# Thirteen single rows per group on SyncE's queue and nine ungathered tiles in a graph-attention kernel

## The chip, the cores and the metric

The kernel runs on one core of one Trainium2 chip. The metric is the device time of one launch in microseconds (us). Before the change the median of three runs is 999.71 us (999.69 to 1000.49).

## What is computed

One layer of graph attention over 6250 nodes and 100000 edges, sorted by destination node, with a residual and a layer norm. Cut to what matters:

```python
Q_h, K_h, V_h = x @ Wq + bq, x @ Wk + bk, x @ Wv + bv      # 6250 nodes, 8 heads of 12
E = edge_attr @ We + be                                     # 100000 edges
score = K_h[src] * Q_h[dst] / sqrt(12) * E
score = exp(clip(score.sum(-1), -5, 5))
wV = segment_sum(V_h[src] * score, dst)                     # edges are sorted by dst
Z = segment_sum(score, dst)
out = layernorm(x + wV / (Z + 1e-6))
```

## The kernel before

The edges are cut into tiles of 128 and the tiles into 99 groups, numbered 0 to 98: 97 groups of eight tiles, then one of four and one of two. Each engine runs the whole series of groups in its own program, unrolled, and semaphores hold the engines together. First a short stage computes K and V for every node and stores them as rows of 768 bytes in a table in DRAM (`kv_table`); Q goes to a second table through the SBUF tensor `q_full`, which nobody uses once the query table is written.

What each engine does per group g:

- **GpSimd (POOL)** gathers K and V of the source nodes: one indirect DMA of 128 rows per tile (line 419), into `kv`, a ring of eight groups. Groups 0 to 3 take another route. Before group g it waits until VectorE has ended group g-8, and from group 16 on also for `q_done` to reach g-1, which is TensorE's end of the query product of group g-2.
- **TensorE (PE)** turns the edge product of group g+1 (line 522), computes the edge projection (line 501) and the query product (line 511) of group g+2, and then sums group g (line 571). The turn of group g+1 needs VectorE's `qe` of g+1.
- **VectorE (DVE)** begins group g with the product of keys and queries (line 944), which needs `kv` of g. Right behind it in its order stands `qe` of group g+1 (line 861), then the reduction, the clip, the messages, and small steps of the layer norm.
- **ScalarE (ACT)** takes the exponential of group g and copies the edge projection of g+2.
- **SyncE (SP)** issues the plain loads. Its turn for group g begins when the query product of g is done (`q_done`, line 355). It then issues two query windows for g+4 (line 244), the edge features of g+4 (line 233) and a row of relations for g+8 (line 228). In every fourth turn, at multiples of four, it first reads eight window bases into registers (line 238), and also issues the load of the residual rows (line 319); in the turn after that it issues the store of an output block (line 330).

Five tiles are not gathered: the last tile of groups 24, 40, 56, 72 and 88 (`BY_ROW`). Their 128 rows are loaded one by one by SP, eight rows at the end of each of 16 successive turns, in turns 7 to 86 (`load_single_rows`, called on line 375): one register load of the eight source nodes (line 341), then eight DMAs of one row each (line 345), into a buffer `kv_rows`. In ACT's program, at the end of group g-1, stands a wait for all 128 rows of group g and a copy of the tile to its place in `kv` (line 696); DVE waits for that copy ahead of line 944 of group g.

Of the kernel before, what the change touches and what calls it, by code (L numbers as in the profile page):

```python
# [4 lines left out]
P = 128  # L5
N = 6250
E = 100000
D = 96
# [12 lines left out]
EPS_LN = 1e-5  # L21
U = 8
CLOSE = 2 * U
BY_ROW = (24, 40, 56, 72, 88)
ROWS = 8
XG = 4
TURNS = NB // U
KV_CHUNKS = (4, 6, 10, 10, 8, 6, 4, 2)
# [33 lines left out]
def gnn_program(nc, xT, xrows, src, src_row, dst_group, dst_tile, eaT, w_node, w_edge, out):  # L62
    f32, bf16, i32 = mybir.dt.float32, mybir.dt.bfloat16, mybir.dt.int32
    ALU, ACT, AX = mybir.AluOpType, mybir.ActivationFunctionType, mybir.AxisListType

    kv_table = nc.dram_tensor("kv_table", (NR, 2 * D), f32, kind="Internal").ap()
# [6 lines left out]
    with ctx:  # L73
        def sb(name, shape, dt):
            return ctx.enter_context(nc.sbuf_tensor(name, shape, dt))
# [23 lines left out]
        q_full = sb("q_full", [P, NR // P, D], f32)  # L99
# [27 lines left out]
        idx = sb("idx", [P, NG * T], i32)  # L127
        ea = sb("ea", [DA, EAR, GE], f32)
        row_id = sb("row_id", [1, len(BY_ROW) * P], i32)
        kv_rows = sb("kv_rows", [P, len(BY_ROW), 2 * D], f32)  # L130
        qwin = sb("qwin", [P, QRING, 2, D], bf16)
        place = sb("place", [P, 2, T, PW], f32)
        qke = sb("qke", [P, T, D], f32)
# [30 lines left out]
        kv_mm, kv_up, kv_out = sem("kv_mm"), sem("kv_up"), sem("kv_out")  # L164
# [8 lines left out]
        row_id_in, rows_up = sem("row_id_in"), sem("rows_up")  # L173
# [30 lines left out]
        def alone(at, t):  # L204

            return at in BY_ROW and t == T - 1

        def engine_turns(eng, body, unrolled):

# [14 lines left out]
        def edge_pass(first):  # L224
# [23 lines left out]
            with nc.Block() as block:  # L248

                @block.sync  # L250
                def _(sp):
# [80 lines left out]

                    ahead = []

                    def load_single_rows(turn):

                        i, j = turn // (P // ROWS), turn % (P // ROWS)
                        if turn == 0:
                            sp.wait_ge(row_id_in, 16)
                            sp.wait_ge(kv_out, 16 * len(KV_CHUNKS))  # L340
                        nodes = nc.values_load_multi_w_load_instructions(
                            row_id[0:1, i * P + j * ROWS:i * P + (j + 1) * ROWS], engines=[sp.engine], min_val=0,
                            max_val=N - 1, skip_runtime_bounds_check_because="source nodes of edges are nodes")[1]
                        for p in range(ROWS):
                            sp.dma_start(kv_rows[j * ROWS + p:j * ROWS + p + 1, i], kv_table[bass.ds(nodes[p], 1), :]
                                         ).then_inc(rows_in[i], 16)

                    def loads(r, k, at):


                        if at >= NG:
                            return
                        g, j, q, half = U * r + k, at % BG, U // BG * r + k // BG, k // BG % 2
                        sp.wait_ge(q_done, g + 1)
                        sp.sem_inc(loads_begun, 1)
                        if j == 0 and at + QRING < NG:
                            ahead[:] = window_rows(sp, g + QRING, min(BG, NG - at - QRING))
                        if at + QRING < NG:
                            load_windows(sp, k % QRING, ahead[2 * j:2 * j + 2])
                        if at + EAR < NG:  # L360
                            load_ea(sp, g + EAR, k % EAR)
                        if at + RELR < NG:
                            load_rel(sp, g + RELR, k % RELR)
                        if not first:
                            return
                        if j == 0 and at < NB:
                            if at >= 2 * BG:
                                sp.wait_ge(block_steps, BLOCK_STEPS * q - 2 * BLOCK_STEPS + 4)
                                sp.sem_inc(stores_begun, 1)
                            load_rows(q, half)  # L370
                        if j == 1 and at >= 2 * BG:
                            store_rows(q - 2, half, at)
                        turn = at - (BY_ROW[0] - P // ROWS - 1)
                        if 0 <= turn < len(BY_ROW) * P // ROWS:
                            load_single_rows(turn)

                    engine_turns(sp, loads, first)
                    if first:
# [334 lines left out]
                def _(dve):  # L713
# [202 lines left out]
                    def arithmetic(r, k, at):  # L916

                        if at == NG:
                            return
                        g = U * r + k  # L920
                        s = k % 2
                        nt = tiles(at)

                        def between(place):


                            step = BLOCK_PLACES.get((at % BG, place))
                            if not first or at < BG or step is None:
                                return
                            if step == BLOCK_STEPS and at >= 3 * BG:  # L930
                                dve.wait_ge(ob_out, 16 * (U // BG) * r + 16 * (k // BG) - 32)
                            block_step(step, U // BG * r + k // BG - 1, 1 - k // BG, BC, xb_in[1 - k // BG], r + k // BG)

                        dve.wait_ge(t_done, g + 1)
                        if first and at < XG:
                            dve.wait_ge(conv_up, T // 2 * (k + 1))
                        else:
                            fills = r if first and k < XG else r + 1
                            singles = sum(1 for x in BY_ROW if first and x <= at and x % U == k)
                            dve.wait_ge(kv_in[k], 16 * (T * fills - (T - nt) - singles))  # L940
                            if first and at in BY_ROW:
                                dve.wait_ge(rows_up, BY_ROW.index(at) + 1)
                        by_bank = dict(b=2, t=nt // 2)
                        nc.vector.tensor_tensor(  # L944
                            qke[:, 0:nt].rearrange("p (t b) d -> p b t d", **by_bank),
                            psT[:, :, 0:nt // 2 * D].rearrange("p b (t d) -> p b t d", d=D),
                            kv[:, k, 0:nt, 0:D].rearrange("p (t b) d -> p b t d", **by_bank),
                            ALU.mult).then_inc(qke_done, 1)
                        if 0 < at < NG - 1:
                            make_qe(r, k + 1, at + 1)  # L950
                        between(0)
                        dve.wait_ge(qke_done, g + 1)
                        nc.vector.tensor_reduce(logit[:, 0:nt * H],  # L953
                                                qke[:, 0:nt].rearrange("p t (h d) -> p (t h) d", h=H), AX.X, ALU.add).then_inc(logit_done, 1)
                        between(1)
                        if at >= 2:
                            dve.wait_ge(wt_done, g - 1)
                        dve.wait_ge(logit_done, g + 1)
                        nc.vector.tensor_scalar(clipped[:, s, 0:nt * H], logit[:, 0:nt * H], -5.0, 5.0, ALU.max,  # L959
                                                ALU.min).then_inc(clip_done, 1)  # L960
                        between(2)
                        if at + 1 < NG and at != NG - 2:
                            make_place(r, k + 1, at + 1)
                        between(3)
                        if at >= 2:
                            dve.wait_ge(sum_done, g - 1)
                        dve.wait_ge(wt_done, g + 1)
                        nc.vector.tensor_copy(weight[:, 0:nt * H].rearrange("p (t h) -> p t h", t=nt),  # L968
                                              msg[:, s, 0:nt, D:ML]).then_inc(weight_held, 1)
                        dve.wait_ge(weight_held, g + 1)  # L970
                        nc.vector.tensor_tensor(  # L971
                            msg[:, s, 0:nt, 0:D].rearrange("p t (h d) -> p t h d", h=H),
                            kv[:, k, 0:nt, D:2 * D].rearrange("p t (h d) -> p t h d", h=H),
                            weight[:, 0:nt * H].rearrange("p (t h) -> p t h", t=nt).unsqueeze(3)
                            .broadcast_to([P, nt, H, HD]), ALU.mult).then_inc(msg_done, 1)
                        if at == NG - 2:
                            make_place(r, k + 1, at + 1)
                        between(4)
                        if at == 0:
                            make_qe(r, k + 1, at + 1)  # L980
                        if at + 3 < NG:
                            make_pick(r, k + 3, at + 3)
                        between(5)
# [122 lines left out]
```

## Time and profile before

| | |
|---|---|
| median of three runs | 999.71 us |
| the profiled execution's own time | 999.58 us |
| its span in the profile | 997.9 us |
| POOL busy | 741.4 us, 74% |
| DVE busy | 651.9 us, 65% |
| PE busy | 646.7 us, 65% |
| ACT busy | 186.5 us, 19% |
| DMA engines, mean busy share | about 0.6 from 150 us on |

The profiled execution is 0.13 us below the median; its span is 1.68 us shorter than its own time. Busy shares count an engine's own work alone. SP has no busy share, since issuing DMAs and loading registers isn't counted; its work is seen in the timeline of its queue. In the timeline, times are microseconds from the start of the span, and a line's second number is how long the merged instructions took.

### The profile page before, as it was taken

What the parts mean: (1) busy time and instruction counts of PE and PEld (TensorE: products, weight loads), DVE (VectorE), ACT (ScalarE), POOL (GpSimd) and SP (SyncE); (2) the same over time, 40 slices, a digit from 0 to 9 for tenths busy, and PEclk for the clock granted to TensorE, in tenths of its full rate; (3) what the DMA queues carried; (4) which work ended last, traced back from release to release, by engine and by line L of the source; (5) the groups of instructions that cost most, each with busy time, mean ns of one, the idle gap of its engine ahead of it and who ended that gap; (6) DMA issues with size and microseconds to landing.
All of it is one profiled execution on the core that took longest, in us unless ns stands there. A gap on an engine that the chain in (4) does not pass through costs nothing. (4 is left out here: it accounts for less than half of the span.)

```text
span 997.9 us, 13968 instructions
## 1 busy us (share of the span) xinstructions
PE 646.7 (65%) x3276; PEld 418.5 (42%) x3276; DVE 651.9 (65%) x1307; ACT 186.5 (19%) x373; POOL 741.4 (74%) x783
## 2 busy tenths in 40 slices
PE   5688778656655665748566666567657664757663
PEld 5564555433433443435333343344434443434443
DVE  6637999666756665766565766566756666657665
ACT  4742222111111111111111111111111111111111
POOL 7777777777777777777777777777777777777772
PEclk9888999888877887886878787877887788887885
DMA  6899776665656556555656556565565565665531
GB/s 196 286 293 244 197 203 176 177 184 156 176 143 170 155 146 177 156 153 159 168 145 167 148 147 171 152 162 156 157 176 142 145 174 149 162 160 140 143 86 42
DMA packets 102425, 165.62 MB, mean 166 GB/s; under 512 B 45725, under 2 KB 65006, under 8 KB 102335
## 3 DMA queue, kind: packets, MB, share of 16 engines
q1 hardware_dynamic: 64399, 84.88, 30.8%
q0 software_dynamic: 36784, 74.86, 28.6%
q10 hardware_dynamic: 1152, 4.92, 1.4%
q8 instruction: 28, 0.46, 0.2%
q14 instruction: 62, 0.51, 0.2%
HBM read 152.18 MB, written 12.39 MB: 165 GB/s over the span
## 5 line engine op out<-in xcount | busy, mean ns | idle before, releaser
L419 POOL DMA_INDIRECT kv<-kv_table,idx x745 | 709.8, 953 | 227.1 <-issue 225.9
L522 PE MATMUL psT<-identity,qe 96*128 96x96 f32 x782 | 111.8, 301 | 292.0 <-DVE qe L861 291.9
L944 DVE TENSOR_TENSOR qke<-psT,kv 128x768 f32<-128x768 f32 (+1 forms) x99 | 93.6, 945 | 288.6 <-DMA kv<-kv_table,idx 287.1
L501 PE MATMUL psE<-ea,we 97*96 97x512 f32 x392 | 268.8, 825 | 0.8 <-ACT kv L641 0.8
L522 PEld LDWEIGHTS psT<-identity,qe 96*128 96x128 f32 x782 | 89.2, 172 | 308.6 <-DVE qe L861 308.4
L571 PEld LDWEIGHTS psA<-place,msg 128*104 128x104 f32 x1536 | 159.9, 179 | 36.0 <-DVE msg L971 26.0
L571 PE MATMUL psA<-place,msg 128*104 128x104 f32 x1536 | 167.0, 264 | 9.9 <-DVE msg L971 9.5
L671 ACT ACTIVATE qe<-psE 96x1024 f32<-96x1024 f32 (+1 forms) x99 | 99.8, 1009 | 231.2 <-PE psE L501 231.2
L685 ACT ACTIVATE msg<-clipped 128x64 f32<-128x64 f32 (+1 forms) x99 | 25.3, 255 | 513.4 <-DVE clipped L959 503.4
L861 DVE TENSOR_TENSOR qe<-psQ,qe 96x1024 f32<-96x1024 f32 (+1 forms) x99 | 118.5, 1197 | 3.7 <-ACT qe L671 3.6
L501 PEld LDWEIGHTS psE<-ea,we 97*96 97x96 f32 x392 | 77.8, 224 | 82.8 <-issue 82.8
L849 DVE TENSOR_TENSOR place<-psI,rel_tile 128x832 f32<-128x832 f32 (+1 forms) x99 | 98.1, 991 | 0.0
L971 DVE TENSOR_TENSOR msg<-kv,psI 128x768 f32<-128x768 f32 (+1 forms) x99 | 93.4, 943 | 3.4
L953 DVE TENSOR_REDUCE logit<-qke 128x64 f32<-128x768 f32 (+1 forms) x99 | 91.4, 924 | 0.0
L511 PE MATMUL psQ<-q_parts,qwin 126*96 126x512 bf16 x196 | 71.3, 450 | 1.2 <-DMA qwin<-q_table 1.2
L511 PEld LDWEIGHTS psQ<-q_parts,qwin 126*96 126x96 bf16 x196 | 30.7, 157 | 87.4 <-issue 85.2
L840 DVE TENSOR_SCALAR q_parts<-q_parts,query_id 126x1024 bf16<-126x1024 bf16 x99 | 50.3, 508 | 15.3 <-DMA q_parts<-rel_table 15.3
L417 POOL DMA_INDIRECT xg<-xrows,idx x32 | 31.0, 969 | 11.1 <-issue 9.4
L959 DVE TENSOR_SCALAR clipped<-logit 128x64 f32<-128x64 f32 (+1 forms) x99 | 21.2, 215 | 4.7
L532 PE MATMUL psA<-identity,accT 104*128 104x104 f32 x73 | 14.8, 312 | 14.4 <-ACT accT L679 13.9
L913 DVE TENSOR_SCALAR ob<-psI,stat,spread 128x96 f32<-128x96 f32 x73 | 23.0, 369 | 0.0
L968 DVE COPY psI<-msg 128x64 f32<-128x64 f32 (+1 forms) x99 | 21.4, 216 | 2.0 <-ACT msg L685 1.9
(105 smaller groups left out, 324.9 us busy)
## 6 DMA issues: line engine op xcount, KB each, us to landing
ea<-eaT SPq DMA_DIRECT2D x99, 384.0 KB, 4.1
q_parts<-rel_table SPq DMA_DIRECT2D x99, 252.0 KB
kv<-kv_table,idx POOLq DMA_INDIRECT x745
kv_rows<-kv_table SPq DMA_DIRECT2D x640, 0.8 KB
qwin<-q_table SPq DMA_DIRECT2D x198, 23.6 KB
xb<-xrows SPq DMA_DIRECT2D x24, 144.0 KB
out<-ob SPq DMA_DIRECT2D x24, 144.0 KB
kv_table<-kv ACTq DMA_DIRECT2D x2, 960.0 KB, 8.3
```

Source lines behind the costliest of these rows:

```text
L419: pool.indirect_dma_start(kv[:, k, t], None, kv_table, sources).then_inc(kv_in[k], 16)
L501: last = nc.tensor.matmul(psE[0:D, h, 0:size], we[:], ea[:, k % EAR, edge:edge + size], start=True, stop=True)
L511: last = nc.tensor.matmul(psQ[0:D, h, 0:size], qwin[0:QR, k % QRING, h], pick[0:QR, k % 2, h * GE // 2:h * GE // 2 + size], start=True, st ...
L522: last = nc.tensor.transpose(psT[:, t % 2, t // 2 * D:(t // 2 + 1) * D], qe[0:D, k % 2, t * P:(t + 1) * P], identity[0:D, 0:D])
L571: last = nc.tensor.matmul(sums[0:ML, off:off + PW], msg[:, s, t], place[:, s, t], start=opens, stop=closes)
L671: nc.scalar.activation(qe[0:D, k % 2, 0:edges], psE[0:D].rearrange("d b e -> d (b e)")[:, 0:edges], ACT.Copy).then_inc(e_up, 1)
L840: nc.vector.tensor_scalar(pick[0:QR, k % 2], rel[0:QR, k % RELR], query_id[0:QR], None, ALU.is_equal).then_inc(pick_done, 1)
L849: nc.vector.tensor_tensor(place[:, k % 2, 0:nt], ps_ids.unsqueeze(1).broadcast_to([P, nt, PW]), rel_tile[:, bass.ds(g * T, nt)].unsqueeze( ...
L861: nc.vector.tensor_tensor(qe[0:D, k % 2, 0:edges], psQ[0:D].rearrange("d b e -> d (b e)")[:, 0:edges], qe[0:D, k % 2, 0:edges], ALU.mult). ...
L944: nc.vector.tensor_tensor(qke[:, 0:nt].rearrange("p (t b) d -> p b t d", **by_bank), psT[:, :, 0:nt // 2 * D].rearrange("p b (t d) -> p b ...
L953: nc.vector.tensor_reduce(logit[:, 0:nt * H], qke[:, 0:nt].rearrange("p t (h d) -> p (t h) d", h=H), AX.X, ALU.add).then_inc(logit_done, 1)
L971: nc.vector.tensor_tensor(msg[:, s, 0:nt, 0:D].rearrange("p t (h d) -> p t h d", h=H), kv[:, k, 0:nt, D:2 * D].rearrange("p t (h d) -> p t ...
```

## The change

- `BY_ROW` is now the last tile of groups 15, 25, 35, ..., 95: nine tiles and not five.
- SP's turns load 13 rows and not 8 (the tenth turn of a tile loads the 11 that are left), so that a tile takes ten turns. They run in turns 4 to 93: turns 4 to 13 load the tile of group 15, turns 14 to 23 that of group 25, and so on. The wait for the table, which stands ahead of the first of them, moves with it from turn 7 to turn 4.
- `kv_rows` lies in `q_full`'s memory.
- POOL's gathers of line 419 go from 745 to 741.
- DVE's wait count for the copy is written as a sum; it means the same.

```diff
-BY_ROW = (24, 40, 56, 72, 88)
-ROWS = 8
+SP_ROWS = 13
+SP_TURNS = -(-P // SP_ROWS)
+FROM = 4
+SP_TILES = tuple(15 + SP_TURNS * i for i in range(9))
+BY_ROW = SP_TILES
...
-        kv_rows = sb("kv_rows", [P, len(BY_ROW), 2 * D], f32)
+        kv_rows = q_full[:].rearrange("p t d -> p (t d)").rearrange("p (i f) -> p i f", f=2 * D)[:, 0:len(BY_ROW)]
...
+        def load_single_rows(eng, i, j, rows):
+
+            count = min(rows, P - j * rows)
+            edge = i * P + j * rows
+            nodes = nc.values_load_multi_w_load_instructions(
+                row_id[0:1, edge:edge + count], engines=[eng.engine], min_val=0, max_val=N - 1,
+                skip_runtime_bounds_check_because="source nodes of edges are nodes")[1]
+            for p in range(count):
+                eng.dma_start(kv_rows[j * rows + p:j * rows + p + 1, i], kv_table[bass.ds(nodes[p], 1), :]
+                              ).then_inc(rows_in[i], 16)
...
-                        turn = at - (BY_ROW[0] - P // ROWS - 1)
-                        if 0 <= turn < len(BY_ROW) * P // ROWS:
-                            load_single_rows(turn)
+                        turn = at - FROM
+                        if turn == 0:
+                            sp.wait_ge(row_id_in, 16)
+                            sp.wait_ge(kv_out, 16 * len(KV_CHUNKS))
+                        if 0 <= turn < len(SP_TILES) * SP_TURNS:
+                            load_single_rows(sp, turn // SP_TURNS, turn % SP_TURNS, SP_ROWS)
...
-                                dve.wait_ge(rows_up, BY_ROW.index(at) + 1)
+                                dve.wait_ge(rows_up, sum(1 for x in BY_ROW if x <= at))
```

## Rows read from the trace of the kernel before

**Rows 1.** Page, costliest groups: out<-in xcount | busy, mean ns | idle before, releaser.
```profile
L419 POOL DMA_INDIRECT kv<-kv_table,idx x745 | 709.8, 953 | 227.1 <-issue 225.9
L944 DVE TENSOR_TENSOR qke<-psT,kv 128x768 f32<-128x768 f32 (+1 forms) x99 | 93.6, 945 | 288.6 <-DMA kv<-kv_table,idx 287.1
```
**Rows 2.** Timeline of POOL: gathers 97, 121, 200, 732; first of groups 16, 19, 29, 96.
```profile
166.57 0.95 POOL L419 DMA_INDIRECT kv<-kv_table,idx  x1 [0.30 <-issue]
...
196.56 0.94 POOL L419 DMA_INDIRECT kv<-kv_table,idx  x1 [0.30 <-issue]
...
295.89 0.95 POOL L419 DMA_INDIRECT kv<-kv_table,idx  x1 [0.30 <-issue]
...
963.03 0.95 POOL L419 DMA_INDIRECT kv<-kv_table,idx  x1 [0.30 <-issue]
```
**Rows 3.** SP's instructions by line: duration ns min/median/max, first and last start.
```profile
L345 SPq DMA_DIRECT2D kv_rows<-kv_table x640: 224/228/288, 116.1 to 871.1; - x160
L341 SPq TENSOR_LOAD <-row_id x80: 526/631/838, 114.8 to 866.8; - x80
L318 SPq TENSOR_LOAD <-block_int x24: 446/462/619, 76.3 to 927.6; - x24
L696 ACT ACTIVATE kv<-kv_rows x5: 350/351/352, 254.6 to 891.3; 128x192 f32<-128x192 f32 x5
```
**Rows 4.** Timeline of SP's queue: turns 4 to 8, turns 13 and 14, and the last of turn 23.
```profile
97.33 0.89 SPq L244 DMA_DIRECT2D qwin<-q_table  x2
98.27 1.79 SPq L233 DMA_DIRECT2D ea<-eaT  x1
100.10 0.41 SPq L228 DMA_DIRECT2D q_parts<-rel_table  x1
101.53 0.37 SPq L319 DMA_DIRECT2D xb<-xrows  x1
102.16 0.87 SPq L244 DMA_DIRECT2D qwin<-q_table  x2
...
103.50 0.40 SPq L228 DMA_DIRECT2D q_parts<-rel_table  x1
106.09 0.84 SPq L244 DMA_DIRECT2D qwin<-q_table  x2
...
112.99 0.85 SPq L244 DMA_DIRECT2D qwin<-q_table  x2
...
114.30 0.41 SPq L228 DMA_DIRECT2D q_parts<-rel_table  x1
116.05 3.15 SPq L345 DMA_DIRECT2D kv_rows<-kv_table  x8
122.26 0.87 SPq L244 DMA_DIRECT2D qwin<-q_table  x2
...
160.45 0.85 SPq L244 DMA_DIRECT2D qwin<-q_table  x2
...
164.66 3.17 SPq L345 DMA_DIRECT2D kv_rows<-kv_table  x8
168.08 0.83 SPq L244 DMA_DIRECT2D qwin<-q_table  x2
...
237.73 3.17 SPq L345 DMA_DIRECT2D kv_rows<-kv_table  x8
```
**Rows 5.** The same view: window loads of turns 12, 16 and 20.
```profile
153.19 0.86 SPq L244 DMA_DIRECT2D qwin<-q_table  x2
...
183.15 0.89 SPq L244 DMA_DIRECT2D qwin<-q_table  x2
...
213.67 0.86 SPq L244 DMA_DIRECT2D qwin<-q_table  x2
```
**Rows 6.** Waits of SP's queue: us in total, times, longest.
```profile
SPq L355 <- PE psQ L511: 253.8, 57, 12.0
```
**Rows 7.** Timeline: DVE's line 944 of groups 4, 15, 16; PE's line 511 of 17.
```profile
100.41 0.95 DVE L944 TENSOR_TENSOR qke<-psT,kv 128x768 f32<-128x768 f32 x1
...
170.85 0.95 DVE L944 TENSOR_TENSOR qke<-psT,kv 128x768 f32<-128x768 f32 x1
...
175.42 0.60 PE L511 MATMUL psQ<-q_parts,qwin 126*96 126x512 bf16 x2
...
179.88 0.96 DVE L944 TENSOR_TENSOR qke<-psT,kv 128x768 f32<-128x768 f32 x1 [3.34 <-DMA kv<-kv_table,idx]
```
**Rows 8.** The same: line 944 of group 22, line 511 of group 24.
```profile
240.15 0.96 DVE L944 TENSOR_TENSOR qke<-psT,kv 128x768 f32<-128x768 f32 x1 [5.90 <-DMA kv<-kv_table,idx]
...
247.03 0.64 PE L511 MATMUL psQ<-q_parts,qwin 126*96 126x512 bf16 x2
```
**Rows 9.** The same: line 944 of groups 95 to 98.
```profile
964.55 0.96 DVE L944 TENSOR_TENSOR qke<-psT,kv 128x768 f32<-128x768 f32 x1 [3.31 <-DMA kv<-kv_table,idx]
974.48 0.96 DVE L944 TENSOR_TENSOR qke<-psT,kv 128x768 f32<-128x768 f32 x1 [4.00 <-DMA kv<-kv_table,idx]
980.25 0.54 DVE L944 TENSOR_TENSOR qke<-psT,kv 128x384 f32<-128x384 f32 x1
983.42 0.35 DVE L944 TENSOR_TENSOR qke<-psT,kv 128x192 f32<-128x192 f32 x1
```
**Rows 10.** Page, DMA issues: KB each, median us to landing.
```profile
ea<-eaT SPq DMA_DIRECT2D x99, 384.0 KB, 4.1
xlast<-xrows SPq DMA_DIRECT2D x1, 48.0 KB, 2.0
```

More of the change, by code:

```diff
@@ L333, in _ @@
                     ahead = []
[L335 to L346, printed above, removed]
                     def loads(r, k, at):
```

## The prediction

> **What bounds the kernel now.** I read the costliest groups first. POOL's gathers are busy for 709.8 us, and every gap before one is "issue": POOL waits for nobody. Line 944 is DVE's only large wait, 287.1 us, and what ends it is the landing of a gather [rows 1]. So the pace is POOL's. The timeline of POOL says how fast that is: from the first gather of group 19 to the first of group 96 there are 611 gathers in 963.03 - 196.56 = 766.47 us, which is 1.254 us each [rows 2]. A gather less is 1.25 us less, as long as nothing makes POOL wait.
>
> This pace doesn't hold from the start. DVE's line 944 walks from group 4 at 100.41 to group 15 at 170.85, 6.4 us per group with no wait, and at group 16 it waits for a gather for the first time [rows 7]. Up to there DVE is catching up with POOL. The new first tile falls just there, in group 15.
>
> Then I read SP's queue, because that is where the new work goes. It waited 253.8 us for TensorE's query product in 57 of its 99 turns [rows 6], so over the whole run it has room. Between turns 12 and 20 it had none: the window loads of turns 12, 16 and 20 stand at 153.19, 183.15 and 213.67, 29.96 and 30.52 us for four turns, back to back, so a turn with eight rows is 7.56 us of pure issuing [rows 5].
>
> **What the change takes away.** Four gathers: 4 x 1.254 = 5.0 us of POOL. The landings of the other tiles stay where they are, later groups move up.
>
> **What it adds on SP.** Eight rows take 3.15 us from first to last [rows 3, 4]; the last alone is 0.23, so one more row is (3.15 - 0.23)/7 = 0.417, of which the first is a little longer: I take 0.41. Five more are 2.05 us. The trace shows no register load of 13 values. One value takes 0.462 us and eight take 0.631 [rows 3], 0.024 per value, so five more are 0.12 if one instruction can carry them, and 0.63 if a second is needed; below nothing it can't be. I take 0.1, the nearer pattern. A full turn so goes from 7.56 to 9.7 us, and since the tenth turn has two rows fewer, ten turns are 10 x 7.56 + 48 x 0.41 + 1.0 = 96.3, with the odd slow issue some 96.7 us. Ten groups at POOL's pace are now 79 x 1.254 = 99.1 us. So SP can just keep pace, at 98% of its time, and makes good only 2.4 us per ten groups of whatever it is behind.
>
> **It begins behind.** The rows of group 15 need ten full turns, 4 to 13, in a stretch where DVE runs a group in 6.4 us and SP would need 8 to 12. Turn by turn, by the window loads [rows 4]:
> - The row part added to a turn that had none is the register load and 13 rows: 0.63 + 0.1 + 12 x 0.41 + 0.23, with small gaps 6.1 us. Turn 4's window load stays at 97.33, since it waits for TensorE; the turn's end, at 101.9, becomes 108.0. Turn 5's window load goes from 102.16 to 108.2.
> - Turns 5 and 6 themselves are 103.90 - 102.16 + 0.25 = 2.0 us, with rows 8.1: the window loads of 6 and 7 come at 116.3 and 124.4, where they were at 106.09 and 112.99.
> - From turn 7's to turn 13's window load it was 160.45 - 112.99 = 47.5 us with eight rows and no wait to speak of; six turns with five more each, 6 x 2.15 = 12.9, give 184.8.
> - Turn 13's rows ended 167.83 - 160.45 = 7.4 us behind its window load; three more rows (it is the turn of 11) make 8.7: the last row of group 15's tile is issued at 193.5.
>
> A single row's landing isn't shown. The nearest is a small load on the same queue, 2.0 us, and the edge loads take 4.1 [rows 10]; I take 2.0. ACT's copy is 0.35 [rows 3], semaphores some 0.15. So DVE can begin group 15 at 193.5 + 2.5 = 196.0 and not at 170.85: **25 us late**. What covers it: `kv` is a ring of eight groups, so DVE's end of group 15 is asked for only by POOL's group 23. What doesn't cover it is the other wait of POOL, q_done. The gathers of group 19 wait for the query product of group 17; that stands in TensorE's program behind the turn of group 16, which waits for `qe` of group 16, which stands in DVE's program behind line 944 of group 15. Before, that chain was 175.42 + 0.60 - 170.85 = 5.2 us long [rows 7]; when TensorE had been idle, from group 22's line 944 to the product for 24, it was 247.67 - 240.15 = 7.5 us [rows 8]. It will have been idle here, so I take 7.5: the product of 17 ends at 203.5, and POOL starts a good 0.2 later, at 203.7. It was due at 196.56 - 1.25 = 195.3 [rows 2], the 1.25 for the tile of group 15. **POOL stalls once for 8.4 us** (6.1 with the short chain).
>
> The edge features and windows for groups 13 to 16 also come late from the same turns; DVE then loses a few us in groups 13 and 14, but group 15 waits longer anyway, so that is inside the 25.
>
> **The next tiles.** The sum needs each of them not to stall POOL again. Turns 14 to 23 ran back to back, 168.08 to 240.90 = 72.8 us [rows 4], plus 9 x 2.15 + 1.3 = 20.7: group 25's last row is issued at about 287.3, DVE begins the group at 289.8, the product of 27 ends at 297.3. POOL is due at group 29 at 295.89 - 1.25 + 8.4 = 303.0 [rows 2]: 5.7 us to spare, and 2.4 more on average with every tile. At the end, turn 93 ends near 193.5 + 80 x 9.67 - 2 (its last turns load less) = 965, so group 95 can begin at 967.5 by its rows; by POOL it begins at 964.55 - 5.0 + 8.4 = 968.0 [rows 9]. That is a tie, and a small lateness there would be taken up, since DVE waits 4.0 us at group 96 anyway [rows 9].
>
> The rest costs nothing. ACT has four more copies of 0.35 us and is 19% busy; while it waits for rows it holds back only what comes after DVE's same wait. The DMA engines move the same bytes. `q_full` is dead by turn 4, so the buffer adds no wait.
>
> **The sum:** -5.0 + 8.4 = +3.4 us on the span, 1001.3; with the 1.68 us around it, 1003.0, and for the median, 0.13 above the profiled execution, 1003.1.
>
> **A rule of the Trainium skill that speaks against this.** "DMA: Bandwidth & Descriptors", section "Issuing engines are not separate DMA queues", says that the time an engine takes to initiate a DMA is usually small relative to the DMA itself. If it were, moving rows to SP would be free. For single rows the trace says otherwise, 0.41 us of SP for 768 bytes [rows 3, 4]. By the page, only the first term of the sum would be left, the third rival below.
>
> **The rivals.**
> - **SP's pace becomes the bound.** Each 0.1 us more per turn makes the last tile's rows 9 us later. For: the tie above, 98% use, the early queue (a load's issue took 1.79 us where 0.37 is usual [rows 4]). Against: DVE's 4 us of room at the end. Beyond the tie, DVE needs 18.9 - 4.0 = 14.9 us from group 95 to 98 and 14.5 to the end of the span. With 0.2 us more per turn: 967.5 + 18 + 14.9 + 14.5 + 1.7 = 1016.6. If the register load must be doubled, 0.63 per turn, it is some 1055. It decides from about 0.05 us more than I count.
> - **Half a stall.** TensorE's chain is short (6.1) or SP's start a little quicker: 999.5 to 1001.7, no change that can be told.
> - **The other side: the late tile is absorbed, and the gain of 5.0 us stands**, 994.7. Place: the first gather of group 19. It happens if DVE begins group 15 by 195.3 - 0.2 - 7.5 = 187.6, 8.4 us sooner than I have it; over the 128 rows of turns 4 to 13 that is 0.065 us per row, 0.35 for 0.41. Against: 640 issues have a minimum of 224 ns and a median of 228 [rows 3], so there is nothing to shrink. For: the walk has ten terms.
>
> **How the numbers follow.** Single stall, 1001.7 to 1006: 0.5. SP's pace, above 1006: 0.22. Half a stall: 0.15. Absorbed or nearly, below 997.7: 0.13. A measurement of this kernel can tell about 0.2%, 2 us, from no change. So faster 0.13, same 0.15, slower 0.72. The range takes in most of the absorbed case and SP's pace up to 0.2 us per turn: 996 to 1017.
>
> **What would show it.** In the new profile: 741 gathers at 1.25 us; one POOL gap of some 8 us ahead of group 19's first gather, released by TensorE's line 511; line 944 of group 15 near 196; row runs of about 5.2 us for 13 rows; SP hardly waiting on line 355 up to about group 60; one register load per turn. I am wrong if POOL has no such gap (absorbed), or if its gaps come back every ten groups and the last line 944s wait for ACT's copy (SP's pace).

## The result

The changed kernel takes **1133.36 us** (median of four runs, 1131.04 to 1136.3), where the kernel before takes 999.7: a ratio of 1.134 with a 95% interval of [1.1313, 1.1367]. It is 134 us slower. The prediction was 1003.1 with a range up to 1017.

The page of the changed kernel. First the busy shares and the two lines that answer to [rows 1], then the chain of work that ended last. After the bar stands the busy time and the mean of one in ns, then the idle time before and what ended it.

```profile
span 1133.1 us, 15518 instructions
...
PE 669.6 (59%) x3276; PEld 428.9 (38%) x3276; DVE 650.1 (57%) x1307; ACT 188.7 (17%) x377; POOL 738.8 (65%) x779
...
SPq 68%; issue 20%; DVE 4%; DMA 3%; PE 3%; ACT 1%; DVEq 0%
SPq L219 29%; SPq L215 18%; SPq L258 6%; SPq L252 4%; SPq L247 3%; SPq L242 3%; PE psE L505 2%; DMA xt<-xT 1%; SPq L339 1%; SPq L332 1%; DVE qe L865 1%; SPq L344 1%; SPq L333 1%; PE psT L526 1%; DMA range_table<-ranges 1%
...
L423 POOL DMA_INDIRECT kv<-kv_table,idx x741 | 705.8, 953 | 343.1 <-issue 213.5
...
L948 DVE TENSOR_TENSOR qke<-psT,kv 128x768 f32<-128x768 f32 (+1 forms) x99 | 92.9, 939 | 166.1 <-ACT kv L700 164.9
```

Every compute engine runs nearly the same instructions as before, in a longer span. (TensorE is busy for 669.6 us and not 646.7, at a mean granted clock of 0.779 and not 0.826; at 59% of the span it isn't what bounds the kernel.) The 741 gathers still take 953 ns each, but POOL now waits between them. DVE's line 948 (944 before) no longer waits for gathers at all: it waits 164.9 us for ACT's copy of the row-loaded tile. And the chain that ended last is now SP's queue: 29% of the span in the row DMAs (line 219) and **18% in one instruction per turn, line 215, the register load of the row ids**. The page of the kernel before follows its chain over some 2% of the span only, so the two chains can't be compared; that POOL set the pace before rests on [rows 1].

SP's instructions by line: duration ns min/median/max, first and last start. They answer to [rows 3].

```profile
L215 SPq TENSOR_LOAD <-row_id x90: 971/2844/3122, 97.1 to 1093.7; - x90
L219 SPq DMA_DIRECT2D q_full<-kv_table x1152: 224/228/287, 98.3 to 1100.9; - x192
```

A row DMA costs what it cost. The load of 13 ids has a median of 2.84 us; I had counted 0.73. There is one per turn, as I had taken for likely, and it is four times too dear. The waits of SP's queue, and three of the other engines (us in total, times, longest):

```profile
SPq L356 <- PE psQ L515: 18.7, 5, 5.8
```
```profile
PE psE L505 <- DMA ea<-eaT: 276.2, 61, 8.9
DVE qe L865 <- ACT qe L675: 257.0, 60, 9.2
POOL kv L423 <- PE psQ L515: 128.0, 37, 11.3
```

SP waited 253.8 us for its turns before [rows 6] and 18.7 now. It is late with everything that it issues, so TensorE waits for edge features, for which it never waited before, DVE waits for the projection of them, and POOL, whose gathers need `q_done`, for TensorE. These are the signs that the prediction named for SP's pace: POOL's gaps come back every ten groups (ahead of groups 16 to 19, 27 to 29, 36 to 39 and so on), and line 948 waits for ACT's copy in all nine groups with a tile loaded by rows, 14.7 to 21.4 us each, up to group 95.

The timeline of SP's queue shows the pace: the window load of turn 14, those of turns 16 and 20 that answer to [rows 5], and that of turn 94.

```profile
204.47 1.14 SPq L258 DMA_DIRECT2D qwin<-q_table  x2
...
226.62 0.86 SPq L258 DMA_DIRECT2D qwin<-q_table  x2
...
272.33 0.87 SPq L258 DMA_DIRECT2D qwin<-q_table  x2
...
1101.42 0.85 SPq L258 DMA_DIRECT2D qwin<-q_table  x2
```

Eighty turns take 1101.42 - 204.47 = 896.95 us, **11.21 us each**, without a wait. POOL needs 9.91 us per group. From turn 94 to the end of the span there are 32 us.

### The profile page after: what moved, and what is told of

It is laid out like the page before. It is cut to its first block, busy times and chain, and to the rows that moved or that the text cites. A ratio compares the mean times of both kernels' runs of the same rounds, so it can differ in the third digit from the quotient of the medians.

```text
span 1133.1 us, 15518 instructions
## 1 busy us (share of the span) xinstructions
PE 669.6 (59%) x3276; PEld 428.9 (38%) x3276; DVE 650.1 (57%) x1307; ACT 188.7 (17%) x377; POOL 738.8 (65%) x779
## 4 chain that ended last, share of the span: by engine, by line
SPq 68%; issue 20%; DVE 4%; DMA 3%; PE 3%; ACT 1%; DVEq 0%
SPq L219 29%; SPq L215 18%; SPq L258 6%; SPq L252 4%; SPq L247 3%; SPq L242 3%; PE psE L505 2%; DMA xt<-xT 1%; SPq L339 1%; SPq L332 1%; DVE qe L865 1%; SPq L344 1%; SPq L333 1%; PE psT L526 1%; DMA range_table<-ranges 1%
## 5 line engine op out<-in xcount | busy, mean ns | idle before, releaser
L505 PE MATMUL psE<-ea,we 97*96 97x512 f32 x392 | 287.6, 875 | 277.0 <-DMA ea<-eaT 276.2
L865 DVE TENSOR_TENSOR qe<-psQ,qe 96x1024 f32<-96x1024 f32 (+1 forms) x99 | 119.1, 1203 | 257.0 <-ACT qe L675 257.0
L575 PEld LDWEIGHTS psA<-place,msg 128*104 128x104 f32 x1536 | 182.1, 198 | 29.5 <-DVE msg L975 13.7
L948 DVE TENSOR_TENSOR qke<-psT,kv 128x768 f32<-128x768 f32 (+1 forms) x99 | 92.9, 939 | 166.1 <-ACT kv L700 164.9
L575 PE MATMUL psA<-place,msg 128*104 128x104 f32 x1536 | 183.7, 280 | 4.9 <-DVE msg L975 4.8
L526 PE MATMUL psT<-identity,qe 96*128 96x96 f32 x782 | 91.0, 263 | 135.6 <-DVE qe L865 135.1
L526 PEld LDWEIGHTS psT<-identity,qe 96*128 96x128 f32 x782 | 76.1, 151 | 145.0 <-DVE qe L865 144.9
L515 PE MATMUL psQ<-q_parts,qwin 126*96 126x512 bf16 x196 | 83.1, 516 | 0.0
L515 PEld LDWEIGHTS psQ<-q_parts,qwin 126*96 126x96 bf16 x196 | 33.5, 172 | 94.7 <-issue 93.8
L963 DVE TENSOR_SCALAR clipped<-logit 128x64 f32<-128x64 f32 (+1 forms) x99 | 23.7, 240 | 4.4
```

Source lines behind the costliest of these rows:

```text
L505: last = nc.tensor.matmul(psE[0:D, h, 0:size], we[:], ea[:, k % EAR, edge:edge + size], start=True, stop=True)
L515: last = nc.tensor.matmul(psQ[0:D, h, 0:size], qwin[0:QR, k % QRING, h], pick[0:QR, k % 2, h * GE // 2:h * GE // 2 + size], start=True, st ...
L526: last = nc.tensor.transpose(psT[:, t % 2, t // 2 * D:(t // 2 + 1) * D], qe[0:D, k % 2, t * P:(t + 1) * P], identity[0:D, 0:D])
L575: last = nc.tensor.matmul(sums[0:ML, off:off + PW], msg[:, s, t], place[:, s, t], start=opens, stop=closes)
L865: nc.vector.tensor_tensor(qe[0:D, k % 2, 0:edges], psQ[0:D].rearrange("d b e -> d (b e)")[:, 0:edges], qe[0:D, k % 2, 0:edges], ALU.mult). ...
L948: nc.vector.tensor_tensor(qke[:, 0:nt].rearrange("p (t b) d -> p b t d", **by_bank), psT[:, :, 0:nt // 2 * D].rearrange("p b (t d) -> p b ...
```

## The experiments

Theory A, formed on seeing line 215: the price of a register load hangs on where in the tensor it begins. The ten turns of a tile begin at values 0, 13, 26, ..., 117; the loads that begin at a multiple of four values (turns 1, 5 and 9 of a tile) took 0.97 to 1.33 us, the six others of 13 took 2.67 to 3.12, and the last of 11 took 2.5 to 2.8. I call the first kind straight and the others crooked. In the kernel before all loads of row ids begin at a multiple of eight. SP's turn against POOL's 9.9 us then decides everything. Rival B: the number of values in a load, 13 against 8. A third: the row DMAs, the buffer in `q_full`, or late edge loads by themselves.

### The price of a register load

`probe_loads` left no trace of itself: its loads, whose values nothing used, weren't in the executed program (13968 instructions, as before).

> The kernel before, with idle register loads of 1 to 16 row ids at several places of row_id added to SyncE's turns 88 to 94, where it waits 10 us and more per group. Theory A (place): a load that begins at a multiple of four values costs about 0.5 us for 8 and 1.0 for 13, one that doesn't costs about 0.22 us per value, 1.8 for 8 and 2.9 for 13. Theory B (number): what counts is 13 against 8 values, the place nothing: 13 at 2.9 us wherever they begin, 8 at 0.53 to 0.8 everywhere. Time unchanged, 999.7 us, by both.

It measured 999.06 us and tells nothing of the theories. With the range checks kept, the values are used:

```diff
+PROBES = {87: ((1, 0), (2, 0)), 88: ((4, 0), (8, 0)), 89: ((12, 0), (13, 0)), 90: ((16, 0), (4, 1)), 91: ((8, 1), (13, 1)),
+          92: ((8, 2), (8, 4)), 93: ((8, 3), (13, 4)), 94: ((13, 8), (12, 4)), 95: ((13, 13), (11, 5)), 96: ((5, 0), (5, 3))}
...
+                        for n, o in PROBES.get(at, ()):
+                            nc.values_load_multi_w_load_instructions(
+                                row_id[0:1, o:o + n], engines=[sp.engine], min_val=0, max_val=N - 1)
```

> The kernel before with register loads of 1 to 16 ids added to SyncE's turns 87 to 96, this time each with its range check, so that they stay in the program; only their own durations matter. Theory A: beginning at a multiple of four values, 0.5 to 0.8 us for up to 8 and 1.0 to 1.2 for 12 to 16; elsewhere 0.22 us per value: 4 at 1.0, 8 at 1.9, 13 at 2.9. Theory B: price by number alone.

The instructions of the probe's line in four short stretches: 4 values from 0; 13 from 0; 8 from 1; 13 from 1.

```profile
L378 SPq TENSOR_LOAD <-row_id x1: 307/307/307, 892.4 to 892.4; - x1
L378 SPq TENSOR_LOAD <-row_id x1: 987/987/987, 903.6 to 903.6; - x1
L378 SPq TENSOR_LOAD <-row_id x1: 1871/1871/1871, 919.1 to 919.1; - x1
L378 SPq TENSOR_LOAD <-row_id x1: 2667/2667/2667, 923.0 to 923.0; - x1
```

All twenty, in ns:

| begins at a multiple of four | | begins elsewhere | |
|---|---|---|---|
| 1, 2, 4, 5, 8 values from 0 | 535, 486, 307, 530, 525 | 4, 8, 13 from 1 | 875, 1871, 2667 |
| 12, 13, 16 from 0 | 749, 987, 1229 | 8 from 2, 8 from 3 | 1669, 2055 |
| 8, 13, 12 from 4, 4, 4 | 530, 987, 758 | 13 from 13, 11 from 5 | 2682, 2280 |
| 13 from 8 | 1164 | 5 from 3 | 1067 |

One count fits them to about 0.1 us: 0.1 us, and 0.22 us for every four values where the load begins at a multiple of four, but 0.2 to 0.22 for **every single value** where it doesn't; what is left over behind the last four also goes one by one (13 is three fours and one, 0.99). Some loads have 0.25 us on top, among the straight ones of the probes those with no register load shortly before. The count also fits the 8 ids of before (0.53 and 0.78), the 13 crooked ones (2.7 to 3.1) and, below, 12 (0.75 and 1.0) and 15 (three fours and three: 1.38 and 1.63). The one-value loads of [rows 3], 0.46 us, lie between its two prices, 0.32 and 0.57. It is a rule fitted to durations; why the place matters no run shows. Theory A holds, with a smaller share of B: straight, 13 ids are 0.99 us and 8 are 0.53.

```diff
-                            row_id[0:1, i * P + j * ROWS:i * P + (j + 1) * ROWS], ...
+                            row_id[0:1, 1 + i * P + j * ROWS:1 + i * P + (j + 1) * ROWS], ...
```

> The kernel before, its row ids shifted by one value, so that each of its 80 loads of eight begins one value past a multiple of four. Theory A: the loads go from 0.63 to about 1.8 us, a turn with rows from 7.56 to 8.8 us, still under POOL's 10.0 per group, so the time stays within 0.2% of 999.7: a price that nobody sees until SyncE is full. Theory B: loads and time unchanged.

Measured: 999.21 us, ratio 0.9991 [0.9982, 1.0001]. The kernel before with all its loads made crooked, its loads by line and its SP queue's wait:

```profile
L341 SPq TENSOR_LOAD <-row_id x80: 1669/1926/2247, 113.8 to 865.4; - x80
```
```profile
SPq L355 <- PE psQ L511: 156.5, 36, 12.3
```

The loads cost three times as much, SP's wait for its turns shrinks from 253.8 to 156.5 us, and the time doesn't move. The trap was there before the change for whoever had moved one id; SP's slack hid it.

### The changed kernel with straight loads

```diff
+PITCH = 16
...
-            edge = i * P + j * rows
+            edge = (i * SP_TURNS + j) * PITCH
```

and the host lays the ids of each turn 16 values apart.

> The changed kernel, the ids of each turn laid 16 values apart, so that every load of 13 begins at a multiple of 16. Theory A: loads go from a mean of 2.3 to 1.1 us, a turn from 11.2 to 10.0 us; SyncE still sets the pace, barely: 1133 less 90 x 1.23 is some 1023 us. Theory B: 1133 us unchanged. A third theory, that the row DMAs or the buffer in q_full's memory cause the loss: 1133 unchanged too.

Measured: 1033.24 us, ratio 1.0334 [1.0316, 1.0351]. 100 of the 134 us are gone. The load's median is 1.22 (mean 1.19), and a turn is (1000.35 - 195.71)/80 = 10.06 us by the window loads of turns 14 and 94. DVE's start of group 15 and POOL's first gather of group 19 come near what I had predicted for the changed kernel:

```profile
L216 SPq TENSOR_LOAD <-row_id x90: 971/1222/1571, 99.9 to 993.6; - x90
```
```profile
197.17 0.96 DVE L949 TENSOR_TENSOR qke<-psT,kv 128x768 f32<-128x768 f32 x1 [17.34 <-ACT kv L701]
...
205.30 0.94 POOL L424 DMA_INDIRECT kv<-kv_table,idx  x1 [7.14 <-PE psQ L516]
...
1000.35 0.83 SPq L259 DMA_DIRECT2D qwin<-q_table  x2
```

DVE begins group 15 at 197.17 (forecast 196.0), and POOL stands still for 7.14 us of which 0.3 is usual: 6.8 (forecast 8.4). The near agreement is partly luck. SP's turn 4 began at 95.26 and not 97.33, its ten turns took 4.0 us more than the 96.2 that I had counted, and from the last row to DVE's start it was 1.7 us and not 2.5; the three cancel but for 1.2 us. And one gap of POOL isn't in the prediction:

```profile
162.94 3.73 PE L506 MATMUL psE<-ea,we 97*96 97x512 f32 x4 [6.97 <-DMA ea<-eaT]
...
166.46 1.06 PE L516 MATMUL psQ<-q_parts,qwin 126*96 126x512 bf16 x2
...
168.30 0.94 POOL L424 DMA_INDIRECT kv<-kv_table,idx  x1 [3.38 <-PE psQ L516]
```

The edge features of group 14 come late, its query product with them, and POOL waits 3.1 us ahead of group 16. Three more gaps follow, ahead of groups 39, 59 and 79, since 10.06 us is still above POOL's 9.91, so SP keeps the pace. What SP is behind at the start it never makes good: DVE begins group 15 by 26.3 us later than before, and 80 turns at 0.15 us too much are 12.0, 38.3 in all. Less the 5.0 us of the gathers this estimate gives 33.3 us, and the kernel is 33.3 us slower than the 999.96 beside it.

> As after_pitch16_load13, but every load takes 16 values (three are not used). Theory A: about 0.75 us per load and a turn of 9.65 us, which is the turn my prediction counted on: SyncE just keeps POOL's pace, one stall of POOL ahead of group 19 of some 8 us, 1003 us. If the loss has another cause than the register loads, it stays far above 1010.

Measured: 1028.68 us, ratio 1.0297 [1.0276, 1.0317], and a turn of 10.03 us. This expectation missed. The load of 16 was no cheaper than that of 13 (both are 0.97 or 1.22 us), which the count above explains: both are four steps. Whether the three unused values were loaded at all the profile doesn't show. As a test of my turn of 9.67 us it failed, so I took the time out of another part of the turn:

```diff
-                    qbase_int[0:1, bass.ds(2 * g, 2 * count)], engines=[sp.engine], min_val=0, max_val=NR - QW)[1]
+                    qbase_int[0:1, bass.ds(2 * g, 2 * count)], engines=[sp.engine], min_val=0, max_val=NR - QW,
+                    skip_runtime_bounds_check_because="window bases are nodes")[1]
```

and the same for the block bases of the loads of line 319 and the stores of line 330 (of before).

> after_pitch16_load13 with SyncE's turns made leaner elsewhere: the range checks of the window and block bases are left out (lines 252, 332, 339), everything else as it is. Some 2 to 3 us per four turns go, so a turn should be 9.4 to 9.6 us instead of 10.05, the turn that my prediction was worked out for. Theory A (SyncE's turn against POOL's 9.91 us per group decides): the loss of 33 us disappears but for one stall of POOL ahead of group 19 of 3 to 8 us, 998 to 1003 us. Rival (row DMAs or late edge loads cost time whatever SyncE's pace): it stays above 1015.

Measured: 997.59 us, ratio 0.9971 [0.9954, 0.9988]. The row DMAs, the tiles, the order and the buffer are those of the changed kernel; a turn is (941.00 - 187.85)/80 = 9.41 us, 3.1 us of waiting in all among the eighty, and 36 us are gone against the turn of 10.06. POOL has one gap:

```profile
193.27 0.95 POOL L427 DMA_INDIRECT kv<-kv_table,idx  x1 [0.31 <-issue]
194.53 0.95 POOL L427 DMA_INDIRECT kv<-kv_table,idx  x1 [0.30 <-issue]
197.23 0.95 POOL L427 DMA_INDIRECT kv<-kv_table,idx  x1 [1.75 <-PE psQ L519]
```

It is the first gather of group 19, released by the query product: the stall of the prediction, but of 1.45 us, because SP began earlier and needed 0.25 us per turn less than I had counted.

### Size and place of the other steps

> pitch16_lean_turn with 15 rows per turn, nine turns per tile and ten tiles (15, 24, ..., 96). Five gathers less are 6.3 us. But a turn goes from 9.37 to about 9.95 us against 71 x 1.254 / 9 = 9.89 of POOL, so SyncE sits on the edge: the debt of the start is never paid back, POOL loses 2 to 6 us in all. 994 to 1000 us; if SyncE's pace were not what decides, 993.

```diff
-SP_ROWS = 13
+SP_ROWS = 15
...
-SP_TILES = tuple(15 + SP_TURNS * i for i in range(9))
+SP_TILES = tuple(15 + SP_TURNS * i for i in range(10))
```

Measured: 1043.34 us, ratio 1.0437 [1.042, 1.0453]. This expectation missed: I had 994 to 1000 us. That SP's turn would lie above POOL's was right, its size not: a turn is 10.27 us and not 9.95, 0.3 of it because 15 ids are six steps and not four. Over 90 turns the 0.38 us above POOL's 9.89 are 34 us. The time is 43 above before, though five gathers (6.3 us) are gone, so some 15 us more were lost; DVE begins group 15 at 185.33, 14.5 us later than before.

> The changed kernel with 12 rows per turn for 13 and the ids packed as they were: eleven turns per tile, eight tiles (16, 27, ..., 93). Every load now begins at a multiple of four values. Theory A: loads at about 1.0 us and a turn of 9.5 us, under POOL's 9.9; three gathers less are 3.8 us, a stall ahead of group 20 of about 2: 998 us. Theory B (the number of values in a load is what makes it dear, 12 being nearly 13): loads near 2.3 us still, a turn of 10.8, above 1070 us.

```diff
-SP_ROWS = 13
+SP_ROWS = 12
...
-SP_TILES = tuple(15 + SP_TURNS * i for i in range(9))
+SP_TILES = tuple(16 + SP_TURNS * i for i in range(8))
```

Measured: 997.13 us, ratio 0.9967 [0.9954, 0.998]. The ids lie packed as in the changed kernel and the checks are kept; what else differs follows from the 12 rows, eleven turns per tile and eight tiles from group 16 on. One row less per turn is 0.41 us; the loads' mean goes from 2.34 to 0.89 us, since every multiple of twelve is one of four. SP waits for its turns again (66.9 us in all, 18.7 in the changed kernel).

```profile
L215 SPq TENSOR_LOAD <-row_id x88: 528/998/1253, 97.4 to 912.9; - x88
```

Now the start. `FROM = 14` and eight tiles from group 25, once with the ids 16 apart, once with the ids packed:

> after_pitch16_load13 with the rows' turns beginning at 14 and not at 4, so that the first tile is that of group 25 and there are eight and not nine. A turn is 10.05 us against 9.91 per group of POOL, so SyncE falls behind by 1.4 us per ten turns, some 11 at the end, from a start without debt; the slack there is about 15. Theory A: no POOL stall at group 19, 999.7 - 3 x 1.25 = 996 us, faster than before. Rival, that SyncE's pace is paid at once: 10.05 against 9.91 over 80 turns is +11, 1007 us.

Measured: 998.11 us, ratio 0.9967 [0.9956, 0.9979], no gap in POOL. A turn is 10.09 us, nearly the one that costs 33 us when rows begin in turn 4. Here SP starts with no debt, falls behind by 0.18 us per turn and ends before the slack does: only the last tiles make DVE wait, 5.6 us in all.

> The changed kernel with its crooked register loads kept, rows' turns from 14 on, eight tiles. A turn of 11.21 us from turn 14 at 157 us on: turn 93 ends at 1054, and the 32 us behind it give 1087. If the early start were what costs, it would be near 996.

Measured: 1082.6 us in a single run. SP's turn 14 begins at 153.2 us and not at 204.2, and those 51.0 us are nearly all that it is faster than the changed kernel, 50.8 by a single run against a median; its turn is still 11.2 us.

> The kernel before with kv_rows in q_full's memory, that part of the change alone. Every theory of mine: no change, 999.7 us; if the place of the buffer had a part in the loss, above 1002.

Measured: 1001.42 us beside 1001.38 of before, ratio 1.0001 [0.9991, 1.0011]. The buffer has no part in it.

Last, the version that the prediction's own arithmetic points to: the lean turn with rows in turns 5 to 94 and the tiles of groups 16, 26, ..., 96.

```diff
-FROM = 4
-SP_TILES = tuple(15 + SP_TURNS * i for i in range(9))
+FROM = 5
+SP_TILES = tuple(16 + SP_TURNS * i for i in range(9))
```

> pitch16_lean_turn with its rows' turns one later, 5 to 94, and its tiles those of groups 16, 26, ..., 96. There DVE began group 15 at 189.3 and POOL lost 1.5 us ahead of group 19. Now group 16's rows are all issued about 9.4 - 5.6 = 4 us later, so that DVE begins it near 193, and POOL needs it, ahead of group 20, 10 us later than before, when 197 is early enough. By my theory no stall: the whole 4 x 1.25 = 5.0 us are gained, 0.995 of the kernel before. Rival, that any tile whose rows come late costs POOL time: no faster than pitch16_lean_turn's 0.997.

Measured: **994.84 us, ratio 0.9948 [0.9934, 0.9962]**. The kernel before is at 999.96 beside it, so the four gathers give back all of their 5.0 us. DVE waits for the first tile as long as ever, and POOL never:

```profile
192.45 0.96 DVE L952 TENSOR_TENSOR qke<-psT,kv 128x768 f32<-128x768 f32 x1 [15.95 <-ACT kv L704]
```
```profile
POOL kv L427 <- PE psQ L519: 0.9, 3, 0.3
```

## Why the prediction was wrong

- **The step that failed** is one term of the sum: the register load of 13 ids. I took a price per value, 0.024 us, from a load of one value and a load of eight [rows 3] and added 0.1 us. Measured, the load is 2.34 us in the mean, 1.61 above the 0.73 of the sum; laid straight it is 1.19, so 1.15 of the 1.61 are the place and 0.46 the number, with the 0.25 that some loads have on top. The loads of eight in [rows 3] all begin at a multiple of eight, where four values cost one step, and the slope drawn from one value to eight hid the step. My upper bound for it, one more load of 0.63, was below the truth as well, so the range missed too. 8 and 13 don't differ in size alone: 13 j is a multiple of four only for every fourth j. That stands in the diff, and I didn't read it there.
- **The Trainium skill had a rule near it** that I didn't weigh: "Runtime: NRT & Kernel Launch", section "Instruction fetch mechanics", says that a register load is about 200 ns per register even in bulk. The page speaks of loads from HBM, the loads here read SBUF. The crooked loads agree (2.67 us for 13, 0.205 each), the straight ones don't (0.525 us for 8, 0.066 each). Worked out from that page, 13 ids would be an estimated 2.6 us.
- **The first rival was right in its mechanism.** It had SP's pace as the bound, with the formula 967.5 + 90 x (excess per turn) + 14.9 + 14.5 + 1.7. The turn was 11.21 and not 9.67: 967.5 + 138.6 + 31.1 = 1137.2, measured 1133.4. I gave it 0.22, and spoke of 1055 only for a second load.
- **The tie was the warning.** The forecast stood on SP being full to 98%, and said that 0.05 us per turn would turn it. With such a margin, a term that no row shows should have carried most of the chance and the range.
- **The stall of POOL** at the first gather of group 19, released by the query product, is seen in both kernels whose turn is near the one that I counted, 9.67: 6.8 us with a turn of 10.06, as the largest of five, and 1.45 with 9.41, as the only one. No kernel with a turn of 9.67 was run. In the changed kernel it is there too, but as one of 27; its first four, ahead of groups 16 to 19, with 0.3 us of each being usual: 

```profile
170.24 0.94 POOL L423 DMA_INDIRECT kv<-kv_table,idx  x1 [4.54 <-PE psQ L515]
...
180.66 0.94 POOL L423 DMA_INDIRECT kv<-kv_table,idx  x1 [0.73 <-PE psQ L515]
...
194.86 0.95 POOL L423 DMA_INDIRECT kv<-kv_table,idx  x1 [4.21 <-PE psQ L515]
...
214.15 0.94 POOL L423 DMA_INDIRECT kv<-kv_table,idx  x1 [9.61 <-PE psQ L515]
```

- **A wait that the prediction put at nothing** is that of group 16. It kept the late edge features and windows of groups 13 to 16 "inside the 25", because DVE waits longer for group 15 anyway. But POOL waits for their query products directly: with the turn of 10.06 us it lost 3.1 us ahead of group 16, in the changed kernel 4.2, and with the turn of 9.41 nothing.
- **The 5.0 us of the four gathers** are real: lean_from5 has them in full.
- **The rule of the Trainium skill that the prediction weighed**, that the time to initiate a DMA is usually small relative to the DMA, doesn't make the moved rows free here: the row DMAs alone are 29% of the chain that ended last. How 0.41 us of issue compares with one row's own DMA no run shows, since a single row's landing isn't in the profile.
- **The cover** of the late first tile, POOL's lead, is shown by pitch16_lean_turn and lean_from5: DVE waits 16.5 and 15.95 us for it, and POOL 1.45 us and nothing.

## What to carry to other kernels

A queue that only issues is an engine with a capacity: before moving work to it, add up its turn, registers and checks included, and compare it with the pace of what bounds the kernel. Below that pace a dear instruction is free (before_off1), above it, once the slack is used up, each tenth of a microsecond is paid in every turn (pitch16_from14 ended before its slack did). When a block size changes, look at what else the old size kept in order, here the place at which a register load begins.

## What the hardware showed that I had not expected

- A register load from SBUF on SP's queue takes 0.1 us and 0.22 per four values if it begins at a multiple of four values of the tensor, and 0.2 to 0.22 per single value if it doesn't, some loads 0.25 more: in the probes 13 values are 0.99 to 1.16 or 2.67 to 2.68 us, 8 are 0.53 or 1.67 to 2.06.
- Leaving out the range checks of ten register values per four turns (eight window bases, two block bases) took a turn from 10.06 to 9.41 us, 0.26 us per check.
- SP's lateness reaches the other engines more by the edge features than by the rows: TensorE waited 276.2 us for them, and DVE 257.0 us for their projection, against 164.9 us for the nine tiles.
